# Taking the first norm and the query, key and value products of an attention block into the slots of two interleaved recurrences

## What is computed

```python
x = x + rnn(x)         # h = tanh(x Wx + b + h Wh), 512 steps
x = x + lstm(x)        # gates i, f, o by sigmoid, g by tanh, 512 steps
x = x + hyperbolic(x)  # attention block on the Poincare ball, conditioned
x = x + experts(x)     # 1 shared and 2 of 4 routed feed-forward experts per sequence
```

```python
ada = cond @ w_ada + b_ada                     # per sequence: sh_msa, sc_msa, g_msa, ...
u  = arctanh(clip(|x|, EPS, MAXT)) * x / |x|   # logmap0
xn = (u - mean(u)) / sqrt(var(u) + 1e-6)
z  = xn * (1 + sc_msa) + sh_msa
q  = (z * min(|z|, ATMAX) / |z|) @ w_q + b_q   # k and v in the same way
```

## Time and profile before

| | |
|---|---|
| median of 3 runs | 2740.08 us (2736.6 to 2740.22) |
| the profiled execution's own time | 2735.61 us |
| its span, first to last instruction | 2733.8 us |
| PE busy (matmuls) | 2212.4 us, 81% |
| DVE busy | 1540.0 us, 56% |
| ACT busy | 1379.0 us, 50% |
| POOL busy | 211.8 us, 8% |
| mean granted clock of PE | 0.976 of full speed |
| DMA | 79.57 MB, mean 29 GB/s |

### The profile page before, as it was taken

One profiled execution on the slowest core, in us unless ns is written; L12 is line 12 of the kernel. 1 busy time (PEld: TensorE's weight loads), 2 busy tenths in 40 slices (PEclk: granted clock), 3 DMA queues, 4 the chain that ended last, 5 costly groups with the idle time before them and its releaser, 6 DMA issues.

```text
span 2733.8 us, 93207 instructions
## 1 busy us (share of the span) xinstructions
PE 2212.4 (81%) x39144; PEld 1538.8 (56%) x39144; DVE 1540.0 (56%) x6664; ACT 1379.0 (50%) x4470; POOL 211.8 (8%) x225
## 2 busy tenths in 40 slices
PE   6777777777777777746488989989989899898999
PEld 5666666666666666622254655646646456365466
DVE  4666666666666666644464555545555556455530
ACT  3444444444444444425346555474464654655542
POOL 0000000000000000001110111111111111011101
PEclk9999999999999999977799999999999999999999
DMA  5000000000000000000001011010010200101110
GB/s 175 14 16 15 12 15 16 16 16 14 15 16 14 14 16 16 8 24 12 0 20 66 1 43 51 27 66 1 27 66 20 74 1 27 66 1 33 49 73 8
DMA packets 96741, 79.57 MB, mean 29 GB/s; under 512 B 74164, under 2 KB 82996, under 8 KB 91588
## 3 DMA queue, kind: packets, MB, share of 16 engines
q1 hardware_dynamic: 93060, 71.09, 8.6%
q10 hardware_dynamic: 3264, 2.52, 0.3%
HBM read 65.16 MB, written 8.44 MB: 27 GB/s over the span
## 4 chain that ended last, share of the span: by engine, by line
PE 40%; ACT 7%; DVE 5%; issue 3%; POOL 0%; DMA 0%; POOLq 0%; ACTq 0%; SPq 0%; DVEq 0%
PE bank L573 12%; PE bank L558 11%; PE bank L760 4%; PE bank L752 4%; ACT pexp L1303 4%; PE bank L661 2%; PE bank L606 1%; PE bank L648 1%; PE bank L590 1%; PE bank L712 1%; PE bank L633 1%; ACT pexp L1233 1%; PE bank L672 1%; DVE big L1004 1%; ACT hidden L1215 1%
## 5 line engine op out<-in xcount | busy, mean ns | idle before, releaser
L130 PE MATMUL psFI<-wh,Hs 128*8 128x128 f32 (+3 forms) x8192 | 325.0, 276 | 307.4 <-DVE Hs L232 307.4
L130 PEld LDWEIGHTS psFI<-wh,Hs 128*8 128x8 f32 (+3 forms) x8192 | 182.3, 99 | 430.6 <-DVE Hs L232 430.6
L130 PE MATMUL psOR<-wh,RH 128*16 128x128 f32 (+3 forms) x8320 | 321.4, 273 | 7.4 <-DMA Hs<-in_condP 3.0
L216 DVE STREAM_TRANSPOSE FIT<-psFI 128x128 f32<-128x128 f32 x512 | 162.3, 317 | 214.3 <-PE psFI L130 213.7
L1303 ACT ACTIVATE pexp<-bank 128x1024 f32<-128x1024 f32 x256 | 242.0, 1022 | 46.5 <-PE bank L648 46.5
L558 PE MATMUL bank<-x3T,ew 128*128 128x512 f32 x512 | 241.2, 596 | 12.2 <-ACT hidden L1215 6.7
L297 ACT ACTIVATE RH<-RT 128x16 f32<-128x16 f32 x512 | 110.8, 216 | 261.0 <-DVE RT L236 261.0
L573 PE MATMUL bank<-ew,hidden 128*128 128x256 f32 x1024 | 239.9, 380 | 0.0
L288 ACT ACTIVATE sFI<-FIT 128x32 f32<-128x32 f32 x512 | 119.0, 232 | 239.1 <-DVE FIT L216 239.1
L573 PEld LDWEIGHTS bank<-ew,hidden 128*128 128x128 f32 x1024 | 193.9, 190 | 76.7 <-issue 54.6
L130 PEld LDWEIGHTS psOR<-wh,RH 128*16 128x16 f32 (+1 forms) x8320 | 205.7, 104 | 10.0 <-issue 5.8
(11 more groups left out here) (246 smaller groups left out, 3949.9 us busy)
## 6 DMA issues: line engine op xcount, KB each, us to landing
ew<-in_ew SPq DMA_DIRECT2D x32, 1024.0 KB, 8.5
XX<-in_xT SPq DMA_DIRECT2D x32, 256.0 KB, 2.7
x_scratch<-x2c SPq DMA_DIRECT2D x32, 128.0 KB, 3.8
z1T<-x_scratch SPq DMA_DIRECT2D x8, 512.0 KB, 3.9
ada<-ada_scratch SPq DMA_DIRECT2D x8, 512.0 KB, 4.8
out_x<-x SPq DMA_DIRECT2D x8, 512.0 KB, 3.3
W_wf<-in_wf SPq DMA_DIRECT2D x2, 1024.0 KB
W_sw<-in_sw SPq DMA_DIRECT2D x2, 1024.0 KB
```

Of the source, the lines that this page charges most:

```text
L130: last = pe.matmul(bank[32 * j:32 * j + width, :], state(k), weights[:, k, j, cols], start=False, stop=k == KC - 1, tile_position=(0, 32 * ...
L216: dve.transpose(flat(R.FIT), R.psFI[g % 2]).then_inc(sem["fiT"], 1)
```

## The change

A new class, `AttentionInputs`, makes the first norm and the q, k, v products for one chunk (128 token rows: 16 steps of 8 sequences) at a time inside the recurrences' loop. Each engine's loop calls `inputs_made(i)` once in each slot: PE between the psOR products and the slot's input products, DVE and ACT at the end of their slot. 32 slots that hold nothing else are put behind the 520. POOL now runs the scalar chain of the norm for each chunk on [128, 1] operands, each operation waiting for the one before; the logarithm is replaced by a 16th root and a series. x with its squared norm, and q, k, v, go to DRAM chunk by chunk and are read back per sequence in the rounds. The conditioning is made in slots 8 to 24. The round -1, the blocks between the loops, and from the rounds everything of the first norm and the q, k, v products, are taken away. The weights of the later stages are loaded one transfer per chunk.

The diff, cut to its core:

```diff
@@ recurrences, PE
                 output_and_rnn(R.psOR[(i // 2) % 2], i, ..., width, R.wh).then_inc(sem["OR"], 1)
+                inputs_made(i)
                 if s == 0:
                     inputs_of_pair(2 * g + 1)
...
+            for i in range(SLOTS, F.END):
+                inputs_made(i)
@@ recurrences, DVE and ACT, at the end of each slot
+                inputs_made(i)
+        @block.gpsimd
+        def _(pool):
+            F.gpsimd_engine(pool)
@@ recurrences, SP
-            for dst, src in W.loads:
-                sp.dma_start(dst, src).then_inc(W.loaded, 16)
+            F.loads(sp)
+            loads = iter(W.loads)
+            for k in range(1, NCH + 4):
+                if k + 2 < NCH:
+                    sp.wait_ge(sem["xx"], 4 * k)
+                    sp.wait_ge(sem["XX"], 8 * k)
+                    sp.dma_start(R.XX[(k + 2) % 3][:, :, :], A["xT"][k + 2]).then_inc(...)
+                F.store_qkv(sp, k - 3)
+                F.store_x(sp, k - 1)
+                for dst, src in itertools.islice(loads, 1):
+                    sp.dma_start(dst, src).then_inc(W.loaded, 16)
+                if k == 1:
+                    F.conditioning_through_dram(sp)
...
+class AttentionInputs:
+    START = Recurrence.LAG + CH
+    END = Recurrence.SLOTS + 2 * CH
...
+    def chunks(self, i):
+        c = (i - self.START) // CH
+        return [(n, i - self.START - CH * n) for n in (c - 1, c) if 0 <= n < NCH]
...
+    def tensor_engine(self, pe, x2, x2_made):
+        def slot(i):
...
+            for c, o in self.chunks(i):
+                if o in (0, 1):
...
+                    last = pe.transpose(columns, x2(c)[:, o, :], self.W.I[:, :])
+                if o in (18, 19):
...
+                    last = pe.transpose(self.psA[:, k * P:(k + 1) * P], self.z[:, k * P:(k + 1) * P], self.W.I[:, :])
+                if 20 <= o < 32:
+                    (n, half), k = divmod((o - 20) // 2, 2), o % 2
...
+                    last = pe.matmul(self.psB[:, half * P:(half + 1) * P], self.zT[:, k, :], self.wqkv[:, k, n * D + half * P:n * D + (half + 1) * P],
+                                     start=k == 0, stop=k == KC - 1, skip_group_check=True)
+    def scalar_engine(self, act):
...
+                if o == 1:
+                    self.raise_(act.copy(self.x[c % 2][:, 0:D], self.psA[:, 0:D]), "xT_out")
+                if o == 15:
+                    self.raise_(act.activation(self.dump[:, :], self.z[:, :], ACT.Square, accum_out=self.S[:, 15:16]), "zz")
+                if o == 19:
+                    self.raise_(act.copy(self.zT[:, :, :].rearrange("p k t -> p (k t)"), self.psA[:, 0:D]), "zT_out")
+    def vector_engine(self, dve):
...
+                if o == 2:
+                    dve.wait_ge(*self.at("xT_out", c))
+                    C.link(dve.bn_stats(self.st6[:, :], self.x[c % 2][:, 0:D]))
+                if o == 3:
...
+                    self.raise_(dve.bn_aggr(self.mv[:, :], self.st6[:, :]), "mv")
+                if o == 5:
+                    dve.wait_ge(*self.at("n", c))
+                    C.link(dve.tensor_scalar(m, n, EPS, MAXT, ALU.max, ALU.min))
+                    self.raise_(dve.tensor_scalar(n, n, EPS, None, ALU.max), "m")
+                if o == 9:
+                    dve.wait_ge(*self.at("d", c))
...
+                if o == 20:
+                    dve.wait_ge(*self.at("nz", c))
...
+                if o == 13:
+                    dve.wait_ge(*self.at("rstd", c))
...
+                    C.link(dve.scalar_tensor_tensor(self.z[:, :], self.x[c % 2][:, 0:D], self.mv[:, 0:1], self.rows[:, 1, :], ALU.subtract, ALU.mult))
+                if o == 14:
+                    self.raise_(dve.scalar_tensor_tensor(self.z[:, :], self.z[:, :], self.S[:, 14:15], self.rows[:, 0, :], ALU.mult, ALU.add), "z")
+                if o in (23, 27, 31):
...
+                    self.raise_(dve.scalar_tensor_tensor(self.qkv[:, cols], self.psB[:, 0:D], s1, self.bqkv[:, cols], ALU.mult, ALU.add), "qkv_out")
+    def gpsimd_engine(self, pool):
...
+        def link(ins):
+            C.link(ins)
+            pool.wait_ge(C.sem, C.n)
+        both = lambda out, x, z, op: link(pool.tensor_tensor(out, x, z, op))
+        scaled = lambda out, x, c0, c1: link(pool.tensor_scalar(out, x, c0, c1, ALU.mult, ALU.add))
...
+        for c in range(NCH):
+            pool.wait_ge(*self.at("mv", c))
...
+            pool.wait_ge(*self.at("m", c))
...
+            pool.wait_ge(*self.at("dk", c))
+            both(t, d, d, ALU.mult)
+            scaled(y, t, 1.0 / 15.0, 1.0 / 13.0)
+            for odd in (11.0, 9.0, 7.0, 5.0, 3.0, 1.0):
+                scaled(y, y, t, 1.0 / odd)
+            both(y, y, d, ALU.mult)
+            both(y, y, k, ALU.mult)
+            both(a, y, rn, ALU.mult)
+            both(t, a, a, ALU.mult)
+            both(t, t, var, ALU.mult)
+            scaled(t, t, 1.0, 1e-6)
+            both(t, t, mhalf, ALU.pow)
+            self.raise_(pool.tensor_tensor(rstd, t, a, ALU.mult), "rstd")
+            pool.wait_ge(*self.at("rstd", c))
+            pool.wait_ge(*self.at("zz", c))
+            self.raise_(pool.tensor_tensor(nz, zz, half, ALU.pow), "nz")
...
 def tensor_round(pe, M, b, front, experts):
-    if front:
-        qkv(0)
-        qkv(1)
     if experts:
         pe.wait_ge(*at("x_out", e))
         transposes(M.x1, (4, 5), "x3T_ps")
     if front:
-        qkv(2)
-        qkv(3)
         steps(0, FC - 1)
...
-    if ahead:
-        raw_transposes()
...
-            if m == 6 and ahead:
-                first_norm_transposes()
 def sync_round(...)
+    def load_qkv(batch):
+        sp.dma_start(M.big[:, :].rearrange("p (q d) -> p q d", q=NQ), tokens(qkv_dram, batch)).then_inc(M.sem("qkv_in"), 16)
+    if b == 0:
+        load_qkv(0)
...
+    if b + 1 < NB:
+        sp.wait_ge(*at("ss_o", b))
+        load_qkv(b + 1)
```

More of the change, by code:

```diff
@@ new lines, in __init__ @@
+        self.ada, self.silu, self.mod = sb("ada", [NB, 6 * D]), sb("silu", [P, KC, NB]), sb("mod", [NB, 2 * E])
+        self.timeb = sb("timeb", [NB, 2 * E])
+        self.wqkv, self.bqkv = sb("wqkv", [P, KC, 3 * D]), sb("bqkv", [P, 3 * D])
+        self.rows = sb("rows", [P, 2, D])
+        self.x, self.z, self.zT = [sb(f"xr_{i}", [P, D + 1]) for i in range(2)], sb("zr", [P, D]), sb("zrT", [P, KC, P])
+        self.dump, self.qkv = sb("dumpr", [P, D]), sb("qkvr", [P, 3 * D])
+        self.st6, self.mv, self.S = sb("st6r", [P, 6]), sb("mvr", [P, 2]), sb("Sr", [P, 16])
@@ new lines, in __init__ @@
+        self.minus, self.root = sb("minus", [P, 1]), sb("root", [P, 1])
+        self.psA, self.psB = (mem.enter_context(nc.psum_tensor(n, [P, 512], fp32)) for n in ("psA", "psB"))
+        self.sig = {n: Signal(nc, ctx, "f_" + n, per) for n, per in self.SIGNALS.items()}
+        one = lambda n: ctx.enter_context(nc.semaphore(n))
+        self.cond_in, self.wada_in, self.wqkv_in, self.sigmoid, self.silu_made, self.mod_ps, self.mod_made, self.ada_ps, self.ada_made, \
+            self.cond_out, self.rows_in, self.mod_in = (one(n) for n in (
+                "cond_in", "wada_in", "wqkv_in", "sigmoid", "silu_made", "mod_ps", "mod_made", "ada_ps", "ada_made", "cond_out", "rows_in", "mod_in"))
@@ L591, in transposes @@
             last.then_inc(M.sem(done), 1)
-    def qkv(q):
-        b0, b1 = (0, 1) if q % 2 == 0 else (2, 3)
-        if q == 0:
-            pe.wait_ge(*at("zT_hi", b))
-            pe.wait_ge(*at("zT_lo", b))
-            if b:
-                pe.wait_ge(*at("ss_f", b - 1))
-        elif q == 1 and b:
-            pe.wait_ge(*at("a", b - 1))
-        elif q >= 2:
-            pe.wait_ge(*at("qkv", b, q - 1))
-        for (lo, hi), bk in (((0, 512), b0), ((512, 768), b1)):
-            for k in range(KC):
-                last = pe.matmul(bank(bk)[:, 0:hi - lo], M.z1T[:, k, q * P:(q + 1) * P], W["wqkv"][:, k, lo:hi], start=k == 0, stop=k == KC - 1)
-        last.then_inc(M.sem("qkv_ps"), 1)
     def gate_logits(bk):
@@ L725, in tensor_round @@
         steps(FC, AFTER_FF)
-    def raw_transposes():
-        pe.wait_ge(*at("x2_in", b + 1))
-        if experts:
-            pe.wait_ge(*at("hidden", e, AFTER_FF))
-        for q in range(NQ):
-            for k in range(KC):
-                columns = bank(4 + q // 2)[:, (q % 2) * D:(q % 2 + 1) * D].rearrange("p (j k u) -> p j k u", k=KC, u=32)[:, :, k, :]
-                last = pe.transpose(columns, M.z1T[:, k, q * P:(q + 1) * P], I[:, :])
-            if q % 2:
-                last.then_inc(M.sem("xT_ps"), 1)
-    def first_norm_transposes():
-        pe.wait_ge(*at("z1", b + 1))
-        transposes(M.z1, (4, 5), "zT_ps")
-    if ahead:
-        raw_transposes()
     if front:
@@ L770, in tensor_round @@
         last.then_inc(M.sem("utot_ps"), 1)
-    elif ahead:
-        first_norm_transposes()
     steps(AFTER_FF, STEPS)
@@ L1410, in gpsimd_round @@
         norm_powers(M.norm2, b, 3)
-    if ahead:
-        for which in (1, 2, 3):
-            norm_powers(M.norm1, b + 1, which)
```

(2 more changed lines are left out.)

492 lines of the change are left out of this document (266 added, 226 removed).

## The result

The changed kernel takes 2642.15 us (median of 4 runs, 2639.58 to 2642.81); the kernel before, run beside it, 2738.34 (2736.03 to 2740.22). The ratio is 0.9647, with a 95% interval from 0.9631 to 0.9664: **96 us or 3.5% faster**. The forecast was 2707 with a range from 2660 to 2765; the result is under the range, and nearest to rival A (2657). The profiled execution took 2642.81 with a span of 2640.8, against a span of 2733.8 before: 93.0 us to be found.

A forecast was written before the change was run, and what follows sets the result against it. PE was taken to bound the rounds, while in the slots, a ring across engines, none is full. -54 - 5 - 7 - 19 + 54.5 = -30.5 from 2735.61 gives 2705.1, put at 2707 us; range 2660 to 2765.

The forecast's parts named there:

- rival A: Slots: the port shared with POOL costs nothing and DVE's excess is small; slots pay 5 us, result 2657; chance 0.20.
- Rounds, -66: Rounds without the q, k, v products: -54 for changes of rounds 2 to 7, -5 round 1, -7 feed-forward transposes.
- Rival D: Rounds give back less, since ACT or DVE sets a round's start: half the 54 us, result 2734; chance 0.06.
- Boundary, -19: From the last x2 to sequence 0's head sums: 42 us instead of 61.0, so 19 us saved.
- Slots, +54.5: The slots pay for the inserted work: 16 + 40 + 1.5 - 3 = 54.5 us slower.
- DVE beside POOL ... +40: Slots: DVE's two-input operations wait for POOL's on the shared port, 40 us slower (0 to 64).
- I take 0.5 ... +16: Slots: DVE's inserted operations exceed its room by 0.5 us a chunk, 32 times, 16 us (range 6 to 35).
- PE at 0: Slots: one transpose or product each; 0.42 us fits PE's room of 0.54, costing nothing.
- ACT at 0: Slots: two copies of about 0.38 us and a square of 0.40 in room of 0.43, costing nothing.
- POOL's chain: Slots, dk to rstd: 15 simple operations and one power take 5.1 us of 9.07, so they fit.
- Early slots at -1.5 net: Early slots: conditioning on DVE costs 1.5 us; taking the burst of weight loads away gives 3 us back.
- Rival B: Slots: POOL late at o = 13, stopping the ring each chunk, if simple operations exceed 0.56 us; 2797 at 0.75; chance 0.14.

The follow-up runs named there:

- The streams: Kernel before with unread POOL operations added in the slots: 1700 one-element powers 2739.90 us, 3600 one-element additions 2750.20, 1250 additions of 256 elements 2821.23, against 2738.21.

## Why the prediction was wrong in the sum and right in two of three parts

**Rounds, -66 against -67.5.** I split a round where DVE has summed the squares of the attention's output over the heads (`ss_t`: `acc` with 4 columns, L1084 before and L1247 after). From these to the next round's head sums, the stretch that holds the change of round, the traces give for each of rounds 2 to 7 105.31 before and 95.33 after: -10.0 each, 60 in all, where 9.0 and 54 were predicted; the second GELU came 10.8 us after the last `down`, not 11.4. Round 1 gave 4.1 (5 predicted). The rest, where the transposes in the feed-forward were to give 7, gave 3.6 net: 2.6 in round 1 and 0.5 in three later rounds, less 0.5 lost in round 0. The two misses nearly cancel, which is luck. Rival D has fallen. The q, k, v loads of later rounds hold up nothing, as costed.

**Boundary, -19 against -23.6.** From the last x2 to z made it took 13.9 (13.4 predicted); from there to the last move 9.1, where transposes, thirds and low clock were to take 9.3; from the last move to the load's issue 2.9, where store and barrier had 5.5; from issue to landing 6.75, where I put 9 by the 1 MB loads of the earlier trace rows; squares and sums 4.8 (4.7). The step that was off is the price of the two transfers, both too high.

**Slots, +54.5 against -1.9.** Here the prediction failed, in two terms; 56 of the 65 us between forecast and result lie here.

*"DVE beside POOL ... +40."* The step took the earlier trace rows, 0.4 of an operation's length lost beside additions of 256 elements, and applied it to operations of one element by their length. The streams show that the length is the wrong measure: 0.067 us for each wide addition of 0.74 us, 0.003 for each power of 0.55. My own sentence "if POOL's tiny operations hardly touch the port, nothing" was the right case, and I gave it (as rival A) 0.20, though the row that I used differed from the operations that I priced by 256 times in data. The Trainium skill (SBUF — State Buffer, "SBUF: two separate sides") has the port pair that the two engines share locked for the whole instruction. For the wide additions the trace agrees in kind: x2, two SBUF inputs, stretched from 0.2 to 0.68 beside additions of 0.74. For a one-element power of 0.55 it does not: gw, scan and Hs stayed within 3 ns and the slots grew by 5.2 us, where the rule would have given some 360. The measurement decides; by the rule the sum would have been 2731, farther from the result than 2707.

*"I take 0.5 ... +16."* The excess is nil. The 0.58 between the starts of x2 and FIT looked like x2's recorded 0.23 us and 0.35 of room, but by the traces after the change x2 holds the engine for only 0.10 of it, and a move for 0.39 of its 0.475. I had priced the overlap on one side (0.415) and read the room by the other. The room was enough, with 0.08 to spare; the doubled move shows the wall behind it.

PE at 0, ACT at 0 and POOL's chain (5.26 against 5.1; threshold 9.07) were right. Early slots at -1.5 net: the changed kernel is ahead by 2.7 us at slot 20 or so, by 1.0 at the FIT of 162.49 (163.53 before) and by 1.9 at the last x2. **Rival B**'s place and mechanism are real, as 24 more operations show, but an operation would have to cost 0.52 and costs 0.28; and its price was too low, since it left out the clock that falls in the stall.

What stays open: whether the 0.003 us that a one-element operation costs at most, by two single runs, goes by operations or by transfers, and how the loss grows between 1 and 256 elements.

## What to carry to other kernels

A slot's room is the distance from start to start, less what each operation holds the engine for; records of VectorE's operations overlap at their ends by 0.08 us here, and idle time in a record understates what fits. Before a contention seen between long operations is carried over to short ones, ask what it scales with, length or data, and if the trace can't say, put the chance on both instead of a number between. A chain on a slow engine with a due time costs nothing up to the due time (8 more operations left the slots as they were), and after it more than the delay (3.5 us of stall, 4.8 of loss a chunk), because PE's clock also fell in the stall.

## What the runs showed that I had not expected

- A POOL power of one element holds POOL for 0.55 us and costs the slots 0.003 or less; an addition of 256 elements of 0.74 us makes an x2 of 0.2 us last 0.68.
- A second product of 128 x 128 in the same place costs PE 0.22 us where the first costs 0.42.
- One load of 1.5 MB lands 6.75 us after its issue; the same in four parts is complete after 8.0 to 8.3.
- A stall of 3.5 us costs on average 1.3 us more behind it: PE's clock fell to 1.2 GHz and came back about six us later in the chunk shown, sooner in most.
